# Windowed attention in a decoder stack: 32 matmuls of 128 contraction rows in place of 64 of 64 rows, for scores and for attention products

## What is computed

```
def local_attention(q, k, v):
    b, h, n, d = q.shape
    w = WINDOW                       # 32
    bq = q.reshape(b, h, nw, w, d)
    ...
    bk2, bv2 = (look(bk), look(bv))  # window before and own window: 64 keys
    ...
    sim = jnp.einsum('bhwie,bhwje->bhwij', bq, bk2) * QK_SCALE
    sim = jnp.where(mask, -jnp.finfo(sim.dtype).max, sim)
    attn = jax.nn.softmax(sim, -1)
    out = jnp.einsum('bhwij,bhwje->bhwie', attn, bv2)

for i in range(DEPTH):               # 6
    x = attn_layer(shift_tokens(x), Wqkv[i], ...) + x
    x = ffn_layer(shift_tokens(x), ln_g[i], ..., W2[i], b2[i]) + x
```

## Time and profile before

| | us |
|---|---|
| median of 3 runs | 1801.8 |
| lowest and highest of them | 1794.27, 1804.09 |
| span of the profiled execution | 1802.4 |
| TensorE matmuls busy | 1631.2 (91%) |
| VectorE busy | 1537.9 (85%) |
| GpSimd busy | 1361.9 (76%) |
| ScalarE busy | 1189.2 (66%) |

### The profile page before, as it was taken

How to read it: one execution, slowest core, us unless ns; L and a number is a source line. 1 busy time by engine, 2 the same in 40 slices (tenths; PEclk the granted TensorE clock), 3 DMA queues, 4 the chain that set the end, 5 groups by cost and what they waited for, 6 DMA issues and landing times.

```text
span 1802.4 us, 77413 instructions
## 1 busy us (share of the span) xinstructions
PE 1631.2 (91%) x32727; PEld 1364.9 (76%) x32727; DVE 1537.9 (85%) x3223; ACT 1189.2 (66%) x2281; POOL 1361.9 (76%) x971
## 2 busy tenths in 40 slices
PE   6688869889899999999999999999999999999996
PEld 4445547778788888788888788887888887888875
DVE  6588679988888998889989899988899998899982
ACT  4455646666676676676668667766777775686763
POOL 4355557788778887778878788887888787788863
PEclk9789979999999999999999999999999999999998
DMA  3644211111311210312212121213112122111111
GB/s 103 257 157 171 77 43 47 44 41 35 102 41 47 60 44 26 108 44 53 55 41 84 53 53 43 61 35 102 41 47 61 44 84 61 41 39 49 40 44 53
DMA packets 81130, 118.48 MB, mean 66 GB/s; under 512 B 41691, under 2 KB 55188, under 8 KB 80660
## 3 DMA queue, kind: packets, MB, share of 16 engines
q1 hardware_dynamic: 80210, 113.27, 21.5%
q10 hardware_dynamic: 578, 0.26, 0.1%
HBM read 38.72 MB, written 21.32 MB: 33 GB/s over the span
## 4 chain that ended last, share of the span: by engine, by line
PE 75%; issue 5%; DVE 4%; POOL 1%; DMA 1%; ACT 0%; SPq 0%; DVEq 0%; ACTq 0%; POOLq 0%
PE banks L1182 10%; PE banks L1195 9%; PE banks L1100 9%; PE banks L1102 7%; PE banks L1101 7%; PE banks L1144 7%; PE banks L1157 5%; PE banks L1122 4%; PE banks L1112 4%; PE banks L1240 4%; PE banks L1212 2%; PE banks L1214 2%; PE banks L1213 2%; PE banks L1083 1%; DVE stream L1644 1%
## 5 line engine op out<-in xcount | busy, mean ns | idle before, releaser
L1436 POOL TENSOR_TENSOR qk_c<-qk_c,qk_s 128x1024 f32<-128x1024 f32 x192 | 459.1, 2391 | 174.8 <-DVE qk_s L1531 174.5
L1444 POOL TENSOR_TENSOR qk_c<-qk_c,nrm 128x1024 f32<-128x1024 f32 x192 | 362.4, 1903 | 60.6 <-DVE nrm L1579 60.6
L1520 DVE TENSOR_TENSOR qk_c<-banks,rot 128x512 f32<-128x512 f32 x384 | 261.9, 682 | 44.8 <-ACT sq L1307 44.0
L1100 PE MATMUL banks<-high,xT 128*128 128x512 f32 x576 | 277.4, 482 | 16.9 <-DVE qk_s L1531 10.7
L1347 ACT COPY pT<-banks 128x512 f32<-128x512 f32 x192 | 112.6, 587 | 226.6 <-PE banks L1157 226.6
L1531 DVE TENSOR_TENSOR qk_s<-banks,rot 128x512 f32<-128x512 f32 x384 | 261.8, 682 | 0.0
L1307 ACT ACTIVATE sq<-banks 128x512 f32<-128x512 f32 x384 | 237.2, 618 | 24.3 <-PE banks L1102 15.3
L1102 PE MATMUL banks<-high,xT 128*128 128x512 f32 x576 | 238.1, 413 | 0.7 <-issue 0.6
L1101 PE MATMUL banks<-low,xT 128*128 128x512 f32 x576 | 236.5, 411 | 0.6 <-issue 0.6
L1538 DVE TENSOR_REDUCE ssq<-sq 128x16 f32<-128x1024 f32 x192 | 232.5, 1211 | 0.0
L1182 PE MATMUL banks<-pT,v_own 64*64 64x32 f32 x6144 | 193.3, 220 | 22.7 <-issue 22.7
(11 more groups left out here) (158 smaller groups left out, 3670.5 us busy)
## 6 DMA issues: line engine op xcount, KB each, us to landing
v_back<-v_own SPq DMA_DIRECT2D x96, 384.0 KB, 3.6
front_raw<-in_L_ffn_Wqkv_dram SPq DMA_DIRECT2D x18, 512.0 KB, 5.5
v_back<-v_own SPq DMA_DIRECT2D x72, 128.0 KB, 2.4
w_high<-high SPq DMA_DIRECT2D x15, 512.0 KB, 2.7
w_low<-low SPq DMA_DIRECT2D x15, 512.0 KB, 4.0
high<-w_high SPq DMA_DIRECT2D x15, 512.0 KB, 5.2
low<-w_low SPq DMA_DIRECT2D x15, 512.0 KB, 6.3
wo<-in_L_ffn_Wo_dram SPq DMA_DIRECT2D x6, 512.0 KB, 5.0
```

The source lines that it names most:

```text
L1100: pe.matmul(bank[n % 2][:, :], xT[:, 1, lo:lo + P], w_hi[:, col:col + 512], start=True, stop=False)
L1436: pool.tensor_tensor(x, x, qk_s[:, kind, :], ALU.add).then_inc(s["rotd"], 1)
L1444: pool.tensor_tensor(x, x, bcast(nrm[:, t % 2, HEADS * kind:HEADS * (kind + 1)], 2, DH), ALU.mult).then_inc(s[("qn", "kn")[kind]], 1)
L1520: dve.tensor_tensor(qk_c[:, t % 2, kind, 512 * half:512 * half + 512].rearrange("p (h d) -> p h d", d=DH), bank[n % 2][:, :].rearrange("p ...
```

## The change

The scores of both heads of a pair and of one window are now made by one matmul of 128 contraction rows. For that, the stationary operand holds the queries of head 0 in its upper left block (64 rows, 32 columns), those of head 1 in its lower right block, and zeros in the other two blocks. The attention products get the same form: for one head, the moving operand holds the probabilities of the two pairs of windows in two diagonal blocks. The operands `qbd` and `pbd` take the place of `qT` and `pT` and are of twice the size. Their zero blocks are set once, before the first round, by two `memset` on GpSimd, for which TensorE and ScalarE wait. The diagonal blocks are filled by ScalarE with two copies of 64 partitions each where one copy of 128 was. The place of a head in the scores' rows changes, and the mask with it. A bank of attention products now holds four pairs of heads and not one half of the tokens.

```diff
-    qT = sb("qT", [P, PAIRS, P])
+    qbd = sb("qbd", [P, PAIRS * GPB, 2, WIN])
...
-    pT = sb("pT", [P, PAIRS, P])
+    pbd = sb("pbd", [P, PAIRS * GPB, 2, WIN])
...
-                for c in range(4):
+                for pair in range(PAIRS):
                     for half_w in range(2):
-                        for par in range(2):
-                            for wpar in range(2):
-                                for hp in range(2):
-                                    pair, w = 2 * c + par, 2 * half_w + wpar
-                                    r = slice(64 * hp, 64 * hp + 64)
-                                    o = 64 * par + WIN * wpar
-                                    last = pe.matmul(
-                                        bank[4 + hp][o:o + WIN, P * c + 64 * half_w:P * c + 64 * half_w + 64],
-                                        qT[r, pair, WIN * w:WIN * w + WIN],
-                                        kT[r, pair, P * j + WIN * w:P * j + WIN * w + 64],
-                                        start=True, stop=True)
+                        for wpar in range(2):
+                            w = 2 * half_w + wpar
+                            o = P * pair + 64 * half_w
+                            last = pe.matmul(
+                                both_scores[64 * wpar:64 * wpar + 64, o:o + 64],
+                                qbd[:, GPB * pair + w, :, :].rearrange("p h q -> p (h q)"),
+                                kT[:, pair, P * j + WIN * w:P * j + WIN * w + 64],
+                                start=True, stop=True)
...
                 for pair in range(PAIRS):
+                    dst = bank[to[pair // 4]][:, P * (pair % 4):P * (pair % 4) + P].rearrange("p (a w q) -> p a w q", a=2, w=2)
                     for wpar in range(2):
-                        for half_w in range(2):
-                            for hp in range(2):
-                                r = slice(64 * half_w, 64 * half_w + 64)
-                                v = (v_own if wpar else v_back)[r, j, DH * (2 * pair + hp):DH * (2 * pair + hp + 1)]
-                                q0 = 64 * (pair % 2) + WIN * wpar
-                                last = pe.matmul(
-                                    bank[to[half_w]][64 * hp:64 * hp + 64, 64 * pair + WIN * wpar:64 * pair + WIN * wpar + WIN],
-                                    v, pT[r, 4 * hp + pair // 2, q0:q0 + WIN], start=True, stop=True)
+                        for hp in range(2):
+                            head = 2 * pair + hp
+                            v = (v_own if wpar else v_back)[:, j, DH * head:DH * head + DH]
+                            last = pe.matmul(dst[64 * hp:64 * hp + 64, :, wpar, :], v,
+                                             pbd[:, GPB * pair + 2 * wpar + hp, :, :].rearrange("p a q -> p (a q)"),
+                                             start=True, stop=True)
...
-                act.copy(qT[:, 4 * half:4 * half + 4, :],
-                         bank[2 + half][:, :].rearrange("p (c t) -> p c t", c=4)).then_inc(s["qT_r"], 1)
+                src = bank[2 + half][:, :].rearrange("p (c q) -> p c q", q=WIN)
+                dst = qbd[:, 16 * half:16 * half + 16, :, :]
+                act.copy(dst[0:64, :, 0, :], src[0:64])
+                act.copy(dst[64:P, :, 1, :], src[64:P]).then_inc(s["qT_r"], 1)
...
-                act.copy(pT[:, 4 * half:4 * half + 4, :].rearrange("p c t -> p (c t)"), bank[2 + half][:, :]).then_inc(s["pT_r"], 1)
+                src = bank[2 + half][:, :].rearrange("p (c q) -> p c q", q=WIN)
+                dst = pbd[:, 16 * half:16 * half + 16, :, :]
+                act.copy(dst[0:64, :, 0, :], src[0:64])
+                act.copy(dst[64:P, :, 1, :], src[64:P]).then_inc(s["pT_r"], 1)
...
-                act.copy(attT[:, :, 64 * half_w:64 * half_w + 64],
-                         bank[(6, 3)[half_w]][:, :].rearrange("p (c t) -> p c t", t=64)).then_inc(s["av_r"], 1)
+                act.copy(attT[:, 4 * half:4 * half + 4, :].rearrange("p c t -> p (c t)"),
+                         bank[(6, 3)[half]][:, :]).then_inc(s["av_r"], 1)
...
+            pool.memset(qbd[:, :, :, :], 0.0).then_inc(s["zeroed"], 1)
+            pool.memset(pbd[:, :, :, :], 0.0).then_inc(s["zeroed"], 1)
```

More of the change, by code:

```diff
@@ L73, in window_masks @@
             for wpar in range(2):
-                rows = slice(hp * 64 + wpar * 32, hp * 64 + wpar * 32 + 32)
+                rows = slice(wpar * 64 + hp * 32, wpar * 64 + hp * 32 + 32)
                 for half in range(2):
@@ L1276, in body @@
                 transpose_k(t - 1, 0)
-            pe.wait_ge(s["zeroed"], 5)
+            pe.wait_ge(s["zeroed"], 7)
             rounds(body)
@@ L1346, in store_prob, with store_att @@
                 need(act, s["av"], t)
-                act.copy(pT[:, 4 * half:4 * half + 4, :].rearrange("p c t -> p (c t)"), bank[2 + half][:, :]).then_inc(s["pT_r"], 1)
-            def store_att(t, half_w):
+                src = bank[2 + half][:, :].rearrange("p (c q) -> p c q", q=WIN)
+                dst = pbd[:, 16 * half:16 * half + 16, :, :]
+                act.copy(dst[0:64, :, 0, :], src[0:64])
+                act.copy(dst[64:P, :, 1, :], src[64:P]).then_inc(s["pT_r"], 1)
+            def store_att(t, half):
                 if not on(t):
@@ L1417, in body @@
                 exponentials(t - 2, 1)
-            act.wait_ge(s["zeroed"], 5)
+            act.wait_ge(s["zeroed"], 7)
             rounds(body)
```

## The result

| | us |
|---|---|
| changed kernel, median of 4 runs | 1921.2 |
| lowest and highest of them | 1920.2, 1921.5 |
| before, in the same comparison, median of 4 | 1802.9 |
| ratio, with its 95% interval | 1.069 [1.066, 1.072] |
| span of the profiled execution (before 1802.4) | 1918.4 |

A forecast was written before the change was run, and what follows sets the result against it. The prediction took TensorE's own work as the bound, VectorE close behind, with TensorE also stopping for late instructions. Its sum was 1802 + 4 + 57 + 48 + 57 - 77 = 1891 us, 5% slower, range 1815 to 1985.

The forecast's parts named there:

- Attention products, 2.00 us as before: TensorE's attention products: 32 records in each of two places take 2.00 us again, low end 1.78.
- Scores, +57 us: TensorE's scores: 2.00 us in place of 1.41, 0.59 us more a tile, 57 us over 96 tiles.
- Zeroing, +4: Two memsets of 128 x 2048 numbers before the first round, hidden by nothing: 4 us.
- The copies' spacing, 0.54 as the middle of 0.48 and 0.60: ScalarE's half copies: each costs as much as a whole one and they follow each other at 0.54 us, ends 0.48 and 0.60.
- First wait, 48 us: TensorE before `transpose_k`, for `store_q` half 0 to read bank 2: 0.32 to 0.69 us a tile, 48 us in all.
- The attention products, both other engines' next inputs, are queued behind it.: TensorE after `transpose_k`: the attention products come later by the wait before it; no wait of their own was given a size.
- Second wait, 57 us for `v_own`: TensorE before `project` of the next tile, behind ScalarE's six copies: 46 to 68 us, 57 as middle.
- The stops, minus 77: TensorE's stops from late instructions and their slow clock all go: minus 77 us, with 39 as the other end.
- The 24 tiles that I took: Tile starts before the change: 373.2 us, 62.2 a row against 59.0 without stops, giving 77 us over 24 rows.
- half copies don't take half the time: Judges the faster rival: on ScalarE a half copy takes half the time, so its waits don't arise; 1786 us, chance 0.10.
- the clock stays at 1.00 beside two waits a tile: Judges the slow-clock rival: new waits bring TensorE's half clock in half of the tiles, 72 us more; 1963 us, chance 0.15.
- places don't stand in line: Judges the rival that TensorE's two places do not overlap: 4.0 us a block, 441 us more; 2275 us, chance 0.04.

The follow-up runs named there:

- attend_only: Kernel before the change with only the attention products in the new form, with half copies of the probabilities; scores and q copies stay old: 1763.9 us, ratio 0.980.
- attend_split: `attend_only` with each attention product of 64 moving columns issued as two of 32: 1917.8 us, ratio 1.067.
- full_copies: Changed kernel with each pair of half copies replaced by a pair of copies of all 128 partitions into the same two slots: 1860.9 us, ratio 1.034.
- single_prob: Changed kernel with one whole copy for each two half copies in `store_prob` only; `store_q` keeps its four half copies: 1849.9 us, ratio 1.028.
- mid_wait: Changed kernel with TensorE waiting for bank 3 only before the fifth pair of heads in the attention products: 1902.9 us, ratio 1.058.
- single_copy: Changed kernel with one copy of 128 partitions for each two half copies, filling only the first slot: 1775.1 us, ratio 0.986.
- wide_scores: Kernel before the change with half its score matmuls, each with 128 moving columns in place of 64: 1730.9 us, ratio 0.963.
- attend_early_q: `attend_only` with the first half of q copied before the third square on ScalarE, not after it: 1760.6 us, ratio 0.978.

## Why the prediction was right, and where its sum was not

The account closes with measured sizes: 1802.9 + 3.8 + 58.6 + 146 - 90 = 1921.3. That it closes to a tenth is chance, since the 146 and the 90 are each good to a few us. Term by term:

- **Attention products, 2.00 us as before: right.** The chain gives `attend` 2.02 us in `attend_only`, for 32 instructions. The change itself is neutral there. That the two full-height places work side by side is shown by it too, and `attend_split` shows that moving columns up to 64 are free there.
- **Scores, +57 us: right.** 2.02 for 1.41 us is 0.61 a tile, 58.6 us.
- **Zeroing, +4: right.** Each memset takes 1.8 us (the earlier trace rows showed the smaller ones), and the first tile's scores start at 261.49 for 257.69, 3.8 us later. This is the line that shows them in the changed kernel:

```profile
231.03 1.80 POOL L1505 MEMSET qbd<- 128x2048 f32 x1
232.78 1.79 POOL L1506 MEMSET pbd<- 128x2048 f32 x1
```

- **The copies' spacing, 0.54 as the middle of 0.48 and 0.60: it was the upper end.** The row of 64 partitions in the earlier trace rows had it right, and the one of 77 in the earlier trace rows was the wrong neighbour. I had both, and mixed them where they disagreed for a reason. The Trainium skill, ScalarE: Activation LUTs, "What ACT_TABLE_LOAD costs", says that successive ACTIVATEs overlap by about 93 ns. For the copies of 128 partitions the traces roughly agree, 0.58 to 0.60 long and 0.47 to 0.48 apart, 0.11 to 0.12 of overlap, and for the half copies they don't, 0.58 long and 0.58 to 0.61 apart. `full_copies` measures the difference in this kernel: 60 us.
- **First wait, 48 us: right place, within its ends.** `transpose_k` starts 0.82 us after the last feed-forward matmul in the tile shown (1316.53 to 1317.35), and 0.24 us after it before (1342.12 to 1342.36): 0.58 us late, 56 us for 96 tiles if all were as this one, and 31 to 66 were given. The bracket shows less, 0.42, since matmuls overlap: idle time counts from the end of one, and the next would have started before that. The copies of the probabilities take part in it, as reckoned: `single_prob` takes it away.
- **The step that failed: "The attention products, both other engines' next inputs, are queued behind it."** They were, but they also have a wait of their own, for bank 3. Half 0 of `store_q` was followed to its bank, half 1 was not; at 0.60 apart it ends 1.20 us later, while `transpose_k` covers 0.53. The products start 1.24 us after `transpose_k` in place of 0.53, 0.71 us late, 68 us for 96 tiles by the tile shown. In the kernel before nothing showed this wait: both q copies had ended at 1342.20, 0.69 us before the products started.
- **Second wait, 57 us for `v_own`: wrong size.** It is 5.8 us in 1300. What I had reckoned as ScalarE's lateness at the end of its six copies was already paid by TensorE at bank 3. `mid_wait`, in which it isn't paid there, has 20.2 us of it in 1200. So it is in part luck that the sum came within 30 us: the wait left out (68 us) and the wait put some 50 us too high largely cancelled. 105 us were forecast for the two waits, and 146 measured for the copies. Of these 56 and 68 are at the two places above; of the other 22 some 7 are the wait for `v_own`, and the rest is not assigned.
- **The stops, minus 77: right that all go, a little small.** No stop is left in the products, and from 400 to 1600 us the granted clock is 1.00 (0.97 before). The first tile's scores start at 257.69 and the last's at 1749.45 in the kernel before, 1491.8 us for 95 tiles, and at the 14.75 us a tile of a row without stops it would be 1401: 90 us. `single_copy`, which has no stops and neither wait, gives nearly the same: 1491.8 and 58 for the slower scores, less its 1457.2, are 93. That all of it is stops and slow clock is inferred, not shown. The 24 tiles that I took were a somewhat quiet stretch. I had half of it as the cautious end, which was not needed.

So of the 30 us that are missing in the forecast, some 41 are the copies and their waits, -13 the stops, and 2 the scores. The rivals fell for the reasons given for them: half copies don't take half the time (0.58 us), the clock stays at 1.00 beside two waits a tile, and places don't stand in line.

The rule on packing (the Trainium skill, TensorE: Matmul & The Clock Gate, "Part 3: Packing small matmuls") was weighed at the scores, with a loss of 84 us to my 57. The measured loss is 58.6: the old block took 1.41 us and not the rule's 0.90. In `wide_scores` half as many matmuls with twice the moving columns each, on the same eight places, take 1.09 us (1305.01 to 1306.10). So the old block was not bound by its moving columns, whose total is the same there; whether the number of instructions or that of weight loads bound it isn't separated, since both are halved.

The better version is a part of the change: `attend_only`, at 1763.9 us, beats both. It takes the attention products, whose two places lose nothing against four, and leaves the scores, whose two places lose 0.61 us a tile against eight. `attend_early_q` is no different from it. `attend_only` still has idle time on TensorE within the scores and the feed-forward part (3.6 and 6.8 us of 1200, "issue"), and waits 13.1 us there for the layers' weights to come in.

## What to carry to other kernels

Before merging small matmuls, count what each array place gets: where the new form has as many records a place, with the same weight columns, as the old one (the attention products, 32 and 32), it costs nothing and saves instructions; where the old form spread over more places (the scores, 16 and 32), it costs. Price the copies that build the block-diagonal operand on the engine that makes them, at the spacing of a row with the same partitions, and follow every bank that these copies free to everyone who takes it, also past the first wait found. An engine that is late by so much pays once: closing one wait moves it to the next, so add up the lateness along the path rather than the waits.

## What was unexpected of the hardware

- ScalarE's copies of 64 partitions don't overlap with what follows: 0.58 us long, 0.58 to 0.61 apart, where 128 partitions of the same 512 elements are 0.48 apart, and the activation of 85 partitions at 1319.01 in the changed kernel lets the next start after 0.57 of its 0.68 us. Halving the partitions made a copy 25% dearer on ScalarE's path. Why was not tried; between 64 and 77 partitions no size was run.
- TensorE's stops depend on where the instructions stand. 262 packets in two kernels went with 38.8 and 9.0 us of stops in the products, 214 in three with none, 11.4 and 25 us. That they are late instructions, how far ahead TensorE's instructions are brought in, and what decides which tile is hit, all stay open.
